# Transposing two layer norms' outputs by crossbar DMA instead of on TensorE

## The reference

```
q  = layer_norm(x) @ wq + bq            # 16 heads of 32
k, v = context @ wk + bk, context @ wv + bv
scores = q k^T / sqrt(32), masked where key position > query position
x1 = x + (softmax(scores) v) @ wo + bo
h  = layer_norm(x1)
out = x1 + gelu(h @ w1 + b1) @ w2 + b2  # w1: 512 x 2048, w2: 2048 x 512
```

## Time and profile before

| | us |
|---|---|
| median of 3 runs | 2116.74 |
| lowest and highest | 2114.98, 2117.86 |
| profiled execution: span from first to last instruction | 2112.4 |
| TensorE matmul busy | 1975.8 |
| VectorE busy | 1304.6 |
| ScalarE busy | 589.0 |
| GpSimd busy | 466.0 |

### The profile page before, as it was taken

One profiled execution on the slowest core, in us unless ns is written; L12 is line 12 of the kernel. 1 busy time (PEld: TensorE's weight loads), 2 busy tenths in 40 slices (PEclk: granted clock), 3 DMA queues, 4 the chain that ended last, 5 costly groups with the idle time before them and its releaser, 6 DMA issues.

```text
span 2112.4 us, 26940 instructions
## 1 busy us (share of the span) xinstructions
PE 1975.8 (94%) x10454; PEld 1003.4 (47%) x10454; DVE 1304.6 (62%) x1972; ACT 589.0 (28%) x820; POOL 466.0 (22%) x380
## 2 busy tenths in 40 slices
PE   4769999999999999999999999999999999999999
PEld 2434445444454544545455444544444454454544
DVE  5876666655656675666666566666655667556642
ACT  3544323222232312223232222313223231222311
POOL 2530131311212141211412023131121214111110
PEclk9879999999999999999999999999999999999999
DMA  7210000101000010000101000010100001000000
GB/s 254 62 28 1 21 20 1 41 0 40 2 11 30 1 41 1 21 20 6 36 1 40 1 21 21 1 40 1 41 1 11 30 1 41 1 21 20 1 21 20
DMA packets 27647, 51.30 MB, mean 24 GB/s; under 512 B 2536, under 2 KB 4112, under 8 KB 27536
## 3 DMA queue, kind: packets, MB, share of 16 engines
q1 hardware_dynamic: 27536, 49.58, 7.1%
HBM read 31.22 MB, written 16.78 MB: 23 GB/s over the span
## 4 chain that ended last, share of the span: by engine, by line
PE 73%; DVE 16%; issue 5%; ACT 3%; DVEq 2%; DMA 0%; POOL 0%; SPq 0%; POOLq 0%; ACTq 0%
PE ff_ps L1190 25%; PE ff_ps L989 23%; PE at_ps L989 15%; PE at_ps L1109 4%; PE at_ps L1032 4%; DVE ssum L927 3%; DVE arena L962 3%; PE at_ps L1133 2%; DVE arena L711 2%; DVEq L688 2%; DVE xhat L707 2%; DVE act_T L711 1%; DVE arena L976 1%; ACT L590 1%; ACT arena L590 1%
## 5 line engine op out<-in xcount | busy, mean ns | idle before, releaser
L1190 PE MATMUL ff_ps<-w_all,arena 128*128 128x512 f16 x3072 | 707.4, 380 | 32.0 <-DVE arena L711 27.7
L989 PE MATMUL ff_ps<-arena,w_all 128*128 128x512 f16 x3072 | 708.5, 381 | 11.9 <-issue 10.3
L1190 PEld LDWEIGHTS ff_ps<-w_all,arena 128*128 128x128 f16 x3072 | 297.8, 98 | 374.2 <-DVE arena L711 30.3
L989 PEld LDWEIGHTS ff_ps<-arena,w_all 128*128 128x128 f16 x3072 | 299.9, 98 | 357.4 <-issue 26.7
L645 ACT ACTIVATE arena<-ff_ps,b1p,scales 128x512 f32<-128x512 f32 x256 | 199.1, 778 | 891.8 <-PE ff_ps L989 803.0
L711 DVE SCALAR_TENSOR_TENSOR arena<-arena,scales 128x512 f16<-128x512 f32 x256 | 285.2, 1114 | 9.1
L485 POOL TENSOR_TENSOR arena<-arena,rsum 128x1024 f32<-128x1024 f32 x64 | 122.7, 1948 | 723.3 <-DVE rsum L930 723.3
L421 POOL TENSOR_TENSOR rstd<-ve,minus_half 128x1 f32<-128x1 f32 x128 | 90.6, 708 | 709.7 <-DVE ve L692 701.4
L962 DVE TENSOR_SCALAR arena<-arena,scales 128x512 f16<-128x512 f32 x256 | 160.1, 625 | 69.3 <-ACT arena L645 69.3
L711 DVE SCALAR_TENSOR_TENSOR arena<-at_ps,arena 128x512 f16<-128x512 f32 x188 | 123.8, 686 | 110.8 <-ACT arena L596 58.5
L989 PE MATMUL at_ps<-wo_hi,act_T 128*128 128x512 f16 x512 | 162.3, 379 | 1.5 <-DVE act_T L711 1.5
(11 more groups left out here) (136 smaller groups left out, 1694.6 us busy)
## 6 DMA issues: line engine op xcount, KB each, us to landing
x_sb<-in_x SPq DMA_DIRECT2D x64, 256.0 KB, 2.6
out_x<-arena SPq DMA_DIRECT2D x64, 256.0 KB, 2.3
w_all<-in_L_xattn_w SPq DMA_DIRECT2D x6, 1024.0 KB, 14.8
arena<-in_L_xattn_w SPq DMA_DIRECT2D x2, 1024.0 KB, 15.0
v_sb<-v_sb SPq DMA_DIRECT2D x6, 192.0 KB, 3.0
arena<-in_ctx SPq DMA_DIRECT2D x1, 1024.0 KB, 5.5
arena<-in_L_xattn_wk SPq DMA_DIRECT2D x1, 1024.0 KB, 8.1
arena<-in_L_xattn_wv SPq DMA_DIRECT2D x1, 1024.0 KB, 8.0
```

The costliest lines, as they stand in the source:

```text
L989: last = nc.tensor.matmul(out_ap, s, m, start=(i == 0), stop=(i == n - 1))
L1190: last = nc.tensor.matmul(ff2_ps[:, t, :], pair[:, s, rows], m[:, j], start=(j == 0 and i == 0), stop=(j == NJ - 1 and i == 2))
```

## The change

The transposes of T and H leave TensorE. ScalarE now reads `xhat` and writes its high fp16 half into a row-major buffer `xhl`, VectorE writes the low half beside it, and SP issues one crossbar transposing DMA per tile: 128 rows of 1024 fp16 values (high and low) to eight blocks of 128 columns in `act_T` or `hT`. `xhl` takes the memory of `qT`. TensorE waits for the four transfers of T before Q0 and for the four of H before the next slot's first FF1 group. `norm_apply` waits for the low half of the tile before in its `xhat` buffer instead of for TensorE. Eight transfers per chunk are added to SP's queue, in a fixed order among its loads and stores. T, Q, S, E, Z, V and O are moved in PLAN by one position for the most part; the probabilities' transposes stay as they are.

```
@@ PLAN
-    2: [("T", 0)], 4: [("T", 1)], 5: [("T", 2), ("T", 3)],
-    6: [("Q", 0)], 7: [("Q", 1)], 8: [("Q", 2)], 9: [("Q", 3)],
-    10: [("S", 0)], 12: [("S", 1)], 13: [("S", 2)], 15: [("S", 3)],
-    16: [("E", 0), ("E", 1), ("E", 2), ("E", 3)],
-    20: [("Z", 0)], 21: [("Z", 1)], 22: [("V", 0), ("V", 1)],
-    23: [("Z", 2)], 24: [("Z", 3)], 25: [("V", 2), ("V", 3)],
-    26: [("O", 0)], 27: [("O", 1)], 28: [("O", 2)], 29: [("O", 3), ("H", 0)],
-    30: [("H", 1)], 31: [("H", 2)], 33: [("H", 3)],
+    2: [("T", 0)], 3: [("T", 1)], 4: [("T", 2)], 5: [("T", 3)],
+    7: [("Q", 0)], 8: [("Q", 1)], 9: [("Q", 2)], 10: [("Q", 3)],
+    11: [("S", 0)], 13: [("S", 1)], 14: [("S", 2)], 16: [("S", 3)],
+    17: [("E", 0), ("E", 1), ("E", 2), ("E", 3)],
+    21: [("Z", 0)], 22: [("Z", 1)], 23: [("V", 0), ("V", 1)],
+    24: [("Z", 2)], 25: [("Z", 3)], 26: [("V", 2), ("V", 3)],
+    27: [("O", 0)], 28: [("O", 1)], 29: [("O", 2)], 30: [("O", 3), ("H", 0)],
+    31: [("H", 1)], 32: [("H", 2)], 33: [("H", 3)],
@@ buffers
-        qT = sb("qT", [P, 2, KT, CHUNK], F16)
+        act_blocks = act_T[:, :, :, :].rearrange("p a k n -> p (a k) n")
+        hT_blocks = [v.bitcast(F16).rearrange("p (b n) -> p b n", n=CHUNK) for v in (hT_a, hT_b)]
+        qT_words = sb("qT", [P, 2 * KT * CHUNK], F16)
+        qT = qT_words[:, :].rearrange("p (a k n) -> p a k n", a=2, k=KT)
+
+        xhl = qT_words[:, :].rearrange("p (t a n) -> p t a n", t=TT, a=2)
@@ SP
+            def move_normed(c, t):
+
+                if t == 0:
+                    wait(sp, o_ps, 4 * c)
+                    sp.sem_inc(moves_begun, 1)
+                sp.wait_ge(t_lo, 4 * c + t + 1)
+                sp.sem_inc(moves_begun, 1)
+                sp.dma_start_transpose(act_blocks[:, :, t * P:(t + 1) * P],
+                                       xhl[:, t].rearrange("p a n -> p (a n)")).then_inc(t_moved[t], 16)
+
+            def move_hidden(c, par, t):
+
+                if t == 0:
+                    wait(sp, ff1_done, NJ * c + (-NJ))
+                    sp.sem_inc(moves_begun, 1)
+                    if isinstance(c, int) and c == 1:
+                        sp.wait_ge(conv_lo, len(conversions))
+                sp.wait_ge(h_lo, 4 * c + t + 1)
+                sp.sem_inc(moves_begun, 1)
+                sp.dma_start_transpose(hT_blocks[par][:, :, t * P:(t + 1) * P],
+                                       xhl[:, t].rearrange("p a n -> p (a n)")).then_inc(h_moved[t], 16)
+
+            for t in range(2):
+                move_normed(0, t)
             move_values(0, slice(0, 2))
+            for t in range(2, TT):
+                move_normed(0, t)
...
+                if attn:
+                    if not first:
+                        for t in range(TT):
+                            move_normed(c, t)
+                    for t in range(TT - 1):
+                        load_next(t)
+                    move_hidden(c, par, 0)
+                    load_next(TT - 1)
+                    for t in range(1, TT):
+                        move_hidden(c, par, t)
@@ ScalarE
+                if kind == "T":
+                    act.wait_ge(ln_out, 8 * c + t + 1)
+                    wait(act, h_moved[t], 16 * c)
+                    nc.scalar.activation(xhl[:, t, 0], xhat[:, t % 2, :], ACT.Copy).then_inc(t_hi, 1)
+                elif kind == "H":
+                    act.wait_ge(ln_out, 8 * c + (TT + t + 1))
+                    act.wait_ge(t_moved[t], 16 * c + 16)
+                    nc.scalar.activation(xhl[:, t, 0], xhat[:, t % 2, :], ACT.Copy).then_inc(h_hi, 1)
@@ VectorE, T (H alike)
-                low(aT_lo[:, :, rows], at_ps[:, t % 2, :].rearrange("p (k n) -> p k n", k=KT), 1.0,
-                    aT_hi[:, :, rows], t_lo)
+                nc.vector.tensor_tensor(xhl[:, t, 1], xhat[:, t % 2, :], xhl[:, t, 0], ALU.subtract).then_inc(t_lo, 1)
@@ TensorE
                         if t == 0:
-                            pe.wait_ge(t_lo, 4 * c + 4)
+                            for n in range(TT):
+                                pe.wait_ge(t_moved[n], 16 * c + 16)
+                            wait(pe, x1_set, 4 * c)
...
                         if g == 0:
-                            pe.wait_ge(h_lo, 4 * c)
+                            for n in range(TT):
+                                pe.wait_ge(h_moved[n], 16 * c)
```

More of the change, by code:

```diff
@@ L265, in cross_attention_block @@
         blk_set = sem("blk_set")
-        (t_ps, q_ps, s_ps, z_ps, v_ps, o_ps, h_ps, ff1_done, ff2_done) = (sem(n) for n in (
-            "t_ps", "q_ps", "s_ps", "z_ps", "v_ps", "o_ps", "h_ps", "ff1_done", "ff2_done"))
+        (q_ps, s_ps, z_ps, v_ps, o_ps, ff1_done, ff2_done) = (sem(n) for n in (
+            "q_ps", "s_ps", "z_ps", "v_ps", "o_ps", "ff1_done", "ff2_done"))
+        moves_begun = sem("moves_begun")
+        t_moved, h_moved = ([sem(f"{n}{t}") for t in range(TT)] for n in ("t_moved", "h_moved"))
         t_hi, t_lo, q_out, q_hi, q_lo, s_max, s_sub, e_set, s_sum, s_rec, p_norm = (sem(n) for n in (
@@ L388, in slot, with load_next @@
             def slot(c, par, attn, ff, batch):
-                if not isinstance(c, int) or c < NCHUNK - 1:
-                    for t in range(TT):
+                first = isinstance(c, int) and c == 0
+                loads = not isinstance(c, int) or c < NCHUNK - 1
+                def load_next(t):
+                    if loads:
                         sp.wait_ge(x1_set, 4 * c + t + 1)
                         sp.dma_start(x_sb[:, t], x_tiles[4 * c + (TT + t)]).then_inc(x_loaded[t], 16)
+                if attn:
[8 more added lines that the diff above has]
+                        move_hidden(c, par, t)
                 if ff:
@@ L902, in step @@
                     bank = at_ps[:, t % 2, :]
-                    tiles = bank.rearrange("p (k n) -> p k n", k=KT)
                     if kind == "T":
@@ L907, in step @@
                         dve.wait_ge(h_hi, 4 * c + t + 1)
-                        rows = slice(t * P, (t + 1) * P)
-                        low(hT[par][:, 1, :, rows], tiles, 1.0, hT[par][:, 0, :, rows], h_lo)
+                        nc.vector.tensor_tensor(xhl[:, t, 1], xhat[:, t % 2, :], xhl[:, t, 0], ALU.subtract
+                                                ).then_inc(h_lo, 1)
                         if t < 2:
@@ L1034, in transposes @@
                 last.then_inc(done, 1)
[L1036 to L1042, removed]
             pe.wait_ge(ctx_lo, KT)
@@ L1052, in _ @@
                                              for k in range(KT)]).then_inc(kv_ps, 1)
-            for t in range(2):
-                T_step(0, t)
             pe.wait_ge(wv_out, KT)
@@ L1067, in values @@
                                              for k in range(KT)]).then_inc(kv_ps, 1)
-            for t in range(2, TT):
-                values(t - 2)
-                T_step(0, t)
+            for n in range(2):
+                values(n)
             pe.wait_ge(conv_lo, CONV_Q)
@@ L1079, in step @@
                     rows = slice(t * P, (t + 1) * P)
-                    if kind == "T":
-                        T_step(c, t)
-                    elif kind == "W":
+                    if kind == "W":
                         values(t)
@@ L1145, in step @@
                                       for k in range(KT)]).then_inc(o_ps, 1)
-                    elif kind == "H":
-                        pe.wait_ge(ln_out, 8 * c + (TT + t + 1))
-                        if t < 2:
-                            pe.wait_ge(x1_set, 4 * c + (t + 3))
-                        else:
-                            pe.wait_ge(h_lo, 4 * c + (t - 1))
-                        transposes(xhat[:, t % 2, :], bank, h_ps)
                 old = hT[1 - par]
```

9 lines of the change are left out of this document (4 added, 5 removed).

## The result

The change makes the kernel slower: median 2178.43 us (2176.28 to 2181.82, 4 runs) against 2117.3 us, a ratio of 1.0296 (95% interval 1.0281 to 1.031). The profiled execution has a span of 2178.2 us, 65.8 us more than before.

The account below looks back on a forecast made before the run. TensorE, busy 94% of the span, was taken as the bound. Slots +94 us, clock +20 and start +12 gave a span of 2238 us, forecast time 2240 us, range 2105 to 2450 us.

Parts of the forecast that it names:

- Most that can be won: TensorE, per slot: removed transposes and waits around T save at most 4.8 us in plain, 8.1 us in batch slots.
- Latency and pace: New transfers on SP's queue: one alone lands after L = 4.4 us, four follow each other every s = 2.5 us.
- lower bound: New transfers priced like ordinary ones of 256 KB: latency 2.6 us, pace 0.8 us by bytes.
- The argument from 1024 short runs: Each transfer writes 1024 runs of 256 bytes; at 87 ns each the pace would be 5.6 us, the upper bound.
- H's wait: TensorE before the next slot's first feed-forward group waits 7.6 us for H's transfers.
- T's wait: TensorE before Q0 waits for T's transfers, 3.9 us in a plain slot and 6.3 us in a batch slot.
- Clock: After the waits TensorE's granted clock falls, adding 1.3 us per slot, +20 us over 15 slots.
- Start: Kernel start, chunk 0: T's transfers add 5 us and H's uncovered ones 7 us, +12 us together.
- Rival 1: Transfers cost what ordinary ones do; the change breaks even at L about 2.7 us or wins, 2107 to 2116; chance 0.22.
- rival 2: The forecast itself: pace from 1.5 to 4 us, about 2150 to about 2390 us; chance 0.56.
- Rival 4: VectorE no longer waits for TensorE's transposes, both waits fall by 1 us, -30 us; chance 0.02 of turning the sign.

Follow-up runs that it names:

- b_plan: The kernel before with only the changed kernel's new table of positions, transposes staying on TensorE: 2077.1 us, ratio 0.9809.
- a_old_table: The changed kernel, T and H by transfers, with the old table of positions: 2219.8 us, ratio 1.0486 to the kernel before.
- b_E17: The kernel before with one edit, the exponentials' step E at position 17 instead of 16: 2089.4 us, ratio 0.9866.
- a_filled: The changed kernel with extra matmuls that compute nothing, 18 before the wait for H's transfers and 10 before T's: 2156.9 us.
- a_T_moved: The changed kernel with H's transposes back on TensorE and T's still by transfers: 2161.0 us, ratio 1.0211 to the kernel before.
- c_cover: The changed kernel with positions moved so seven feed-forward groups stand before Q0 and four after O3: 2091.4 us, ratio 0.9873 to the kernel before.
- c_cover2: The changed kernel with positions moved so seven feed-forward groups stand before Q0 and five after O3: 2145.5 us, ratio 1.0132 to the kernel before.

## Why the prediction was right in sign and twice too large

- **Direction and range**: slower was forecast with 0.78, and 2178 lies in 2105 to 2450 and in the forecast's own 2150 to 2390. The time over the kernel before was forecast as +123 us and measured as +61. That the time came out inside the range is in part luck, since errors of both signs stand below.
- **The step that failed** is "Most that can be won: 4.8 us per plain slot, 8.1 us per batch slot". It prices the removed transposes and the waits around T, and gives the moved table no value. Shown by b_plan and by a_old_table against the changed kernel: the table is worth 40 us, 28 of them from E's step alone (b_E17). It removed the 1.93 us wait behind Z once per slot. Without the table's gain the transfers cost 103 us, near the 123 us forecast; this too is partly luck, for latency and pace were too high and the clock's price too low.
- **Latency and pace** were taken too high: L 4.4 against 3.1, s 2.5 against 1.24 us. The lower bound (2.6 and 0.8) was nearer than the upper one: a short packet cost 22 ns, not 87. The argument from 1024 short runs failed; SP's issue sets how fast transfers can follow each other (1.23 us, and nearly the same for half the data), and no row of before showed it for such a transfer. The sentence of the Trainium skill ("Advanced Engine Details and Errata", X-Bar Transpose (TRN2)) that such transfers are as fast as regular ones was closer than my middle: 3.1 against 2.6 us to landing, though with 1.23 us of issue against SP's 0.33 for a load (line 392 of the kernel before). The 1309 ns per block of "VectorE: DVE Perf Modes" (The three transpose paths), also the Trainium skill, taken eight times, an estimate of 10.5 us, is far from the 3.1 us of this case.
- **H's wait**: 7.6 forecast, 4.1 (plain) and 6.0 us (edge) measured. **T's wait**: 3.9 and 6.3 forecast, 2.5 and 4.5 measured. In plain slots H's is short by about what L and s were high; VectorE's low was placed well, H3's at X + 8.4 forecast and 9.0 measured, and with the measured L the prediction's own arithmetic gives 9.0 + 3.1 - 7.8 = 4.3 us. For T two errors cancel: T3's low half ends at S + 17.5 and not 14.4, and TensorE is ready at S + 18.4 and not 15.5. The first groups at the low clock hold up both, TensorE itself and the gelu pairs that stand ahead of the lows; in a_filled, at the full clock, the low ends at S + 15.5.
- **Clock**: forecast 1.3 us per slot, too little. In the two slots shown the three groups behind H's wait lose 2.3 and 2.7 us (10.11 and 10.49 to the next group's start, against 7.78), which a_filled shows to be the clock; T's wait absorbs a part.
- **Start**: forecast +12; the first feed-forward group starts at 150.32 instead of 140.55, +9.8.
- **Rival 1** named break-even at L = 2.7 and was judged by L alone. At 3.1 its formulas give 2 x 3.1 - 0.5 - 4.8 = +0.9 and 2 x 3.1 + 2.5 - 8.1 = +0.6 us per slot. For two slots the rest is H's wait 0.4 and 2.3 us longer than the formulas have it, T's 0.5 longer and 0.5 shorter, and the low clock with 6.3 us, less 3.6 us behind Z: +6.9. So even with the latency known these formulas leave out the clock, the slower landing at the loop's edge and the table's gain.
- **The forecast's lower end** (rival 2, "At s = 1.5 ... about 2150") leaves out the clock: its waits give +29 us in the slots, and with the 20 us of the forecast's own clock term and a few for the start it comes to about 2170.
- **Rival 4**, VectorE's slack: the lead exists, but H's wait gives it. Once that wait is gone, T3's low in a batch slot ends 2.5 us later (a_T_moved).

**The account for two slots**, from the rows shown: removed, transposes 2 x 3.45 = 6.9, waits around T 1.3 + 3.2, at the loop's edge 1.5, behind Z 2 x 1.8: 16.5 us. Added, H 4.1 + 6.0, T 2.5 + 4.5, low clock in the first groups 2.7 + 2.3 and in Q of the batch slot 1.3: 23.4 us. Net +6.9; measured 257.9 - 250.3 = +7.6. Times 7.5, with 9.8 us at the start, this gives 62 to 67 us for the 65.8 us.

**The best version** among those run is b_plan, the kernel before with the new table: 2077.1 us, 1.9% under the kernel before and 4.7% under the changed kernel. The best one with transfers, c_cover, needs 2091.4 us, and loses its time to b_plan at the kernel's start.

**Open**: why H's last transfers take longer at the loop's edge (below), whether TensorE's transposes would still win with c_cover's table, and which of the moved positions besides E bring b_plan's last 12 us.

## What to carry to other kernels

A change that moves work between engines and reorders the schedule at once is two changes: time the new order with the old engines before crediting or blaming the rest. A transposing transfer frees TensorE of 0.43 us per tile but puts its whole landing time behind the last input, so it pays only where more independent work than that latency (here 3.1 us, and VectorE's lag before it) stands between the last tile and its reader; and the idle time can cost more than its length, because the clock can fall in it. Count cover, the independent work between the last input and its reader, at both ends of the loop together. Moving the border from one end to the other only passed the wait on (a_old_table against the changed kernel); taking two positions out of the middle brought 87 us (c_cover), and a third put a new wait there (c_cover2).

## What the runs showed of the hardware

- SP needs 1.23 us to issue a transposing transfer of 256 KB and 1.19 us for one of 128 KB; the plain loads in the earlier trace rows land after 2.6 us, these after 3.1 and 2.4 us. At the loop's edge single issues took up to 2.69 us.
- At the loop's edge H's last transfers land later. The DMA view of two windows of the changed kernel (queue, kind: packets, MB, share; transfers, median us to landing); the first lies at a loop's edge, the second at a plain slot's end, where no instruction packets are listed:

```profile
q8 instruction: 2, 0.03, 1.7%
arena<-qT SPq DMA_TRANSPOSE x3, 4.4
```

```profile
q1 hardware_dynamic: 3393, 1.21, 87.4%
arena<-qT SPq DMA_TRANSPOSE x3, 3.1
```

  In the ten slot ends looked at, the instruction queue moves two packets in the five at a loop's edge, where the landing takes 3.9 to 4.4 us, and none in the five others, where it takes 3.1 or 3.2 us. That they are the cause was not tried.
- A short wait is not tied to one clock: in c_cover the three groups behind a wait of 2.56 us took 9.45 us at a granted clock of 0.83, and in the same run behind one of 2.61 us they took 7.94 us. TensorE's work ahead of the two waits is the same table, so the length of the wait alone does not say which level follows.
- VectorE's low-half pass from SBUF took 0.68 us at the median, 0.78 us in the mean for T (`L911`) and 0.91 us for H (`L953`), with single ones up to 1.76 us, the slow ones that were looked at beside GpSimd (301.74 us). So moving its source from PSUM to SBUF cost little on the whole: VectorE's busy time grew from 1304.6 to 1315.3 us.
